# Mean squares of a fused transformer block: square sums turned by TensorE and added up by VectorE

## Chip, cores, metric

One core of one Trainium2 chip. The metric is the device time of one launch, in microseconds; the median of the runs is compared. PE is TensorE, DVE VectorE, ACT ScalarE, POOL GpSimd.

## The reference

128 sequences of 64 tokens with 256 features pass a conditioned layer norm, attention with 16 heads and a gated feed-forward network. Two of its steps are RMS norms, one ahead of attention and one ahead of the network:

```
xhat = layernorm(x) * w + b + tanh(cond @ lin_w.T + lin_b);  x = xhat * w + b
norm(x, t) = gamma(t) * x * rsqrt(mean(x * x, axis=-1) + 1e-6) + beta(t)
x = x + a_alpha(t) * attention(norm_a(x, t))
x = x + f_alpha(t) * swiglu(norm_f(x, t))
```

## The kernel before

The 8192 tokens are worked on in 32 parts of 256 tokens (four sequences). Features lie on the partitions (two halves of 128, `KT`), tokens along the free axis. All engines run one static list of slots `s` from -8 on. A slot does one sequence of attention scores (`s`), the exponentials, the turned probabilities of sequence `s-2`, the product with the values of `s-3`, and one quarter (step `f = s - 12`) of the feed-forward work of a part. Four slots make a group (`grp = s // 4`, `j = s % 4`); each engine goes through the list in order, and semaphores tie them together.

The norms of two parts share the group: part `grp + 2` for attention and part `grp - 2` for the network. Groups -2 to 1 have the first only, groups 2 to 29 both, groups 30 to 33 the second only. Their way:

- j = 0: TensorE turns the input of part `grp + 2` (`turn_x`, L310, four transposes). VectorE makes the residual (L576). ACT squares both parts (L763, L769), POOL adds the two feature halves (L949, L955), so that `square_sum_a` and `square_sum_f` are 128 partitions x 256 tokens.
- j = 1: `mean_squares` (L318, L323): for each block of 128 tokens a product with the square sums as the stationary operand and the column `mean_col` (all 1/256) as the moving one, which leaves the mean of each token on a partition, in columns 0 to 3 of `norm_bank`. VectorE adds epsilon to the 128 x 4 numbers (`mean_squares_out`, L626) and signals `ms_out`; POOL raises them to -1/2 (`inverse_rms`, L942).
- j = 2: `spread_inverses` (L331): one transpose per block of a column broadcast along 128, after which `norm_bank` holds the inverse of each token on all partitions; VectorE multiplies with it (`scale_by_rms`, L629).

`norm_bank` is PSUM bank 1, the bank that `hidden` fills in every slot from 12 on. So TensorE waits in `norm_bank_read` for whoever reads the bank for the norm before `hidden` writes it: at j = 1 for `ms_out`. Large products are done as three fp32r products of high and low halves (`three_pass`, L280 to L282).

In the list of TensorE a slot with j = 1 is: `turn_probs` (L408), `times_values` (L419), `score` (L397), `mean_squares`, 12 products of `queries`, 12 of `gate`, 12 of `hidden`, 12 of `down` (L468, L472 to L474; the first of a part is 512 columns wide, L468, and clears the bank). VectorE has in such a slot: `product_lo` (L666), `find_least` (L584), `mean_squares_out` (L626), `gate_ffn` (L674), `activate` (L652, waits for ACT's tanh, L845), `invert_sums` (L600, L605), `product` (L660), and in every second group statistics (L532, L539 to L549). ACT has `probs_out` (L830), then the exponentials (L822, eight), tanh (L845), `queries_out` (L796) and `product_hi` (L851). POOL has `normalise_probs` (L1002), `inverse_rms` (L942), in every second group `normalise_tokens` (L994), and `add_ffn` (L1011).

Of the kernel before, what the change touches and what calls it, by code (L numbers as in the profile page):

```python
# [28 lines left out]
ALU = mybir.AluOpType  # L29
ACT = mybir.ActivationFunctionType  # L30
F32 = mybir.dt.float32
F32R = mybir.dt.float32r
AX_X = mybir.AxisListType.X

P = 128
BATCH, SEQ, D = 128, 64, 256
# [11 lines left out]
NC = 4  # L48
VW = 2 * DH
SCALE = (HEADS / D) ** 0.5  # L50
LN_EPS, RMS_EPS = 1e-5, 1e-6

SHIFT, A_GAMMA, A_BETA, A_ALPHA, F_GAMMA, F_BETA, F_ALPHA = range(7)
# [14 lines left out]
def conditioned_block(nc, x, cond_t, mod_w, feat_vecs, attn_w, gate_w, hidden_w, out_w, identity, head_mask, out_t):  # L68
    with ExitStack() as ctx:
        def sb(name, shape, dt=F32):  # L70
            return ctx.enter_context(nc.sbuf_tensor(name, shape, dt))

        def sem(name):
            return ctx.enter_context(nc.semaphore(name))
# [4 lines left out]
        turn_bank, norm_bank, work = bank[0], bank[1], bank[7]  # L79
# [5 lines left out]
        vecs = sb("vecs", [P, 4, KT])  # L85
        w_sq = sb("w_sq", [P, KT])
        ident = sb("ident", [P, P])
        mean_col = sb("mean_col", [P, 1])
        minus_half = sb("minus_half", [P, TILES])
        mask = sb("mask", [P, 4])  # L90
        pair = sb("pair", [P, 2])
# [13 lines left out]

        squares_a = sb("squares_a", [P, KT, PART])
        square_sum_a = sb("square_sum_a", [P, PART])
        mean_sq = sb("mean_sq", [P, 4])
        normed_a = sb("normed_a", [P, KT, PART])
        xn_hi = sb("xn_hi", [P, KT, PART], F32R)  # L110
# [9 lines left out]
        probsT = [sb(f"probsT{i}", [P, NC * P]) for i in range(2)]  # L120
# [4 lines left out]
        squares_f = sb("squares_f", [P, KT, PART])  # L125
        square_sum_f = sb("square_sum_f", [P, PART])
# [24 lines left out]
        stats_made, merged, var_made, rstd_made = sem("stats_made"), sem("merged"), sem("var_made"), sem("rstd_made")  # L151
        x_normed, x_turned, res_made = sem("x_normed"), sem("x_turned"), sem("res_made")
        squared_a, sq_sum_a, squared_f, sq_sum_f = sem("squared_a"), sem("sq_sum_a"), sem("squared_f"), sem("sq_sum_f")
        ms_mm, ms_out, inv_made, inv_spread = sem("ms_mm"), sem("ms_out"), sem("inv_made"), sem("inv_spread")
        gamma_a, scaled_a, xn_a = sem("gamma_a"), sem("scaled_a"), sem("xn_a")
        hi_a, lo_a = sem("hi_a"), sem("lo_a")
        k_mm, k_out, q_mm, q_out, v_mm, v_out = (sem("k_mm"), sem("k_out"), sem("q_mm"), sem("q_out"),
# [15 lines left out]
        def is_part(m):  # L173
            return 0 <= m < NPART

        def is_seq(g):
            return 0 <= g < BATCH
# [7 lines left out]
        def is_group(grp):  # L185
            return is_part(grp + 2) or is_part(grp - 2)

        def norm_step(s):
            return 3 if s == -2 else 2 if s == -1 else s % PSEQ
# [16 lines left out]
        def res_part(m):  # L206
            return x_res[:, m // 2 % RES, :, m % 2 * PART:(m % 2 + 1) * PART]
# [70 lines left out]
        def _(pe):  # L278
# [12 lines left out]
            def norm_bank_read(j, grp):  # L291
                if j == 0 and is_part(grp + 2):
                    pe.wait_ge(res_made, 2 * (grp + 2) + 2)
                if j == 1 and is_group(grp):
                    pe.wait_ge(ms_out, grp + 3)
                if j == 2 and is_part(grp + 2):
                    pe.wait_ge(scaled_a, grp + 3)
                if j == 2 and is_part(grp - 2):
                    pe.wait_ge(scaled_f, grp - 1)

            def norm_bank_free(s):
                norm_bank_read(norm_step(s - 1), (s - 1) // PSEQ)
                if s - FFN_AT >= 1:
                    pe.wait_ge(prod_made, min(s - FFN_AT, FFN_STEPS))
# [6 lines left out]
                                          xin[m // 2 % 2][:, m % 2 * 2 + i, kt * P:(kt + 1) * P], ident[:])  # L311
                mm.then_inc(x_turned, 1)

            def mean_squares(grp):
                if is_part(grp + 2):
                    pe.wait_ge(sq_sum_a, grp + 3)
                    for i in range(2):
                        mm = pe.matmul(norm_bank[:, i:i + 1], square_sum_a[:, i * P:(i + 1) * P], mean_col[:],  # L318
                                       start=True, stop=True)
                if is_part(grp - 2):  # L320
                    pe.wait_ge(sq_sum_f, grp - 1)
                    for i in range(2):
                        mm = pe.matmul(norm_bank[:, 2 + i:3 + i], square_sum_f[:, i * P:(i + 1) * P], mean_col[:],  # L323
                                       start=True, stop=True)
                mm.then_inc(ms_mm, 1)

            def spread_inverses(grp):
# [28 lines left out]
            def queries(m):  # L356
                if m >= 1:
                    pe.wait_ge(k_out, m + 1)
                project(WQ, m).then_inc(q_mm, 1)
# [22 lines left out]
            def score_banks_free(s):  # L382
                if is_seq(s - 1):
                    pe.wait_ge(scores_read, s)
                if s % PSEQ == 3 and is_part(s // PSEQ - 1):
                    pe.wait_ge(att_lo_made, s // PSEQ)
# [14 lines left out]
            def turn_probs(g):  # L401
                pe.wait_ge(probs_made, g + 1)
                if g >= 1:
                    pe.wait_ge(probsT_out, g)
                if g + 2 - FFN_AT >= 1:
                    pe.wait_ge(act_made, g + 2 - FFN_AT)
                for r in range(4):
                    mm = pe.transpose(turn_bank[:, r * P:(r + 1) * P], probs[g % 2][:, r * P:(r + 1) * P], ident[:])  # L408
                mm.then_inc(probs_turned, 1)
# [72 lines left out]
            for s in range(FIRST_SLOT, LAST_SLOT):  # L482
                grp, j, f = s // PSEQ, s % PSEQ, s - FFN_AT
                if is_seq(s - 2):
                    turn_probs(s - 2)
                score_banks_free(s)
                if is_seq(s - 3):
                    times_values(s - 3)
                if is_seq(s):
                    score(s)  # L490
                norm_bank_free(s)
                if j == 0 and is_part(grp + 2):
                    turn_x(grp + 2)
                if norm_step(s) == 1 and is_group(grp) and s >= 0:
                    mean_squares(grp)
                if norm_step(s) == 2 and is_group(grp) and s >= -4:
                    spread_inverses(grp)
                if s == FIRST_SLOT + 1:
                    mean_squares(grp)
                if s == FIRST_SLOT + 2:  # L500
                    spread_inverses(grp)
                if s == FIRST_SLOT + 1:
                    pe.wait_ge(rest_loaded, 16)
                    modulation(A_BETA, 2)
                if s == FIRST_SLOT + 2:
                    modulation(F_GAMMA, 3)
                if s == 0:
                    values(0)
                if j == 0 and is_part(grp + 1):
                    keys(grp + 1)  # L510
                if j == 1 and is_part(grp + 1):
                    queries(grp + 1)
                if s == FIRST_SLOT + 5:
                    mean_squares(grp)
                if j == 2 and 1 <= grp + 1 < NPART:
                    values(grp + 1)
                if j == 3 and is_part(grp - 1):
                    attention_out(grp - 1)
                if is_step(f):
                    gate(f)  # L520
                    hidden(f)
                if is_step(f - 1):
                    down(f - 1)

        @block.vector
        def _(dve):
# [94 lines left out]
            def mean_squares_out(grp):  # L621
                dve.wait_ge(ms_mm, grp + 3)
                if grp >= -1:
                    dve.wait_ge(inv_spread, grp + 2)
                cols = norm_cols(grp, 1)
                dve.tensor_scalar(mean_sq[:, cols], norm_bank[:, cols], RMS_EPS, None, ALU.add).then_inc(ms_out, 1)  # L626

            def scale_by_rms(normed, first):
                return dve.tensor_tensor(normed[:], normed[:],  # L629
# [76 lines left out]
            for s in range(FIRST_SLOT, LAST_SLOT):  # L706
                grp, j, f = s // PSEQ, s % PSEQ, s - FFN_AT
# [50 lines left out]
        def _(act):  # L758
            def square_a(m):
                act.wait_ge(res_made, 2 * m + 2)  # L760
                if m >= 1:
                    act.wait_ge(sq_sum_a, m)
                act.activation(squares_a[:], res_part(m), ACT.Square).then_inc(squared_a, 1)  # L763

            def square_f(m):
                act.wait_ge(resid_made, m + 1)
                if m >= 1:
                    act.wait_ge(sq_sum_f, m)
                act.activation(squares_f[:], res_part(m), ACT.Square).then_inc(squared_f, 1)  # L769

            def split_hi_a(m):
                act.wait_ge(xn_a, m + 1)
# [19 lines left out]
            def queries_out(m):  # L792
                act.wait_ge(q_mm, m + 1)
                if m >= 2:
                    act.wait_ge(scored, PSEQ * (m - 1))
                act.activation(q_heads[:, m % 2].rearrange("p k s t -> p (k s t)"), proj_bank(WQ, m), ACT.Copy, scale=-SCALE  # L796
                               ).then_inc(q_out, 1)
# [69 lines left out]
                    act.activation(split_cols(w_hi, w), raw_weight(w), ACT.Copy).then_inc(w_hi_made, 1)  # L867

            act.wait_ge(consts_set, 1)
            act.activation(probsT[0][:, 0:1], mean_col[:], ACT.Tanh)  # L870
            act.wait_ge(loaded, 16 * 3)
            act.wait_ge(mod_mm, 1)
            for kt in range(KT):
# [7 lines left out]
            for s in range(FIRST_SLOT, LAST_SLOT):  # L881
                grp, j, f = s // PSEQ, s % PSEQ, s - FFN_AT
# [45 lines left out]
        def _(pool):  # L928
# [81 lines left out]
                pool.wait_ge(gated_f_made, m + 1)  # L1010
                pool.tensor_tensor(res_part(m), res_part(m), gated_f, ALU.add).then_inc(y_made, 1)  # L1011

            pool.memset(mean_col[:], 1.0 / D)
            pool.memset(minus_half[:], -0.5).then_inc(consts_set, 1)
            pool.memset(v_diag[:], 0.0).then_inc(v_cleared, 1)
            pool.wait_ge(consts_set, 1)
# [1 line left out]
            for s in range(FIRST_SLOT, LAST_SLOT):  # L1018
                grp, j, f = s // PSEQ, s % PSEQ, s - FFN_AT
# [72 lines left out]
```

## Time and profile before

| | |
|---|---|
| runs | 1029.57 us median of 3 (1027.64 to 1029.68) |
| profiled execution | 1028.54 us, span 1026.7 us, mean granted clock 0.985 |
| busy | PE 986.7 us (96%), DVE 668.0 (65%), ACT 624.8 (61%), POOL 565.1 (55%) |

Times are microseconds from the start of the span. The busy time of PE includes the pipelines' depth, so the start of the next instruction is what tells the cost of one. Rows are quoted as the profile and the trace give them.

### The profile page before, as it was taken

How to read it: one execution, taken by the hardware profiler on the slowest of the kernel's cores; microseconds unless marked ns; L12 is line 12 of the kernel's file. 1: busy time of each engine (PE TensorE's matmuls, PEld its weight loads, DVE VectorE, ACT ScalarE, POOL GpSimd, SP SyncE). 2: the span in 40 equal slices, each digit the busy share in tenths (PEclk: the TensorE clock that was granted, in tenths of full speed). 3: DMA queues.
4: the chain of work that ended last, by engine and by line, in shares of the span. 5: the costliest groups of instructions: out<-in, count | busy, mean ns of one | idle time of the engine just before them, and what ended most of it. 6: DMA issues, size and time to landing. Idle time of an engine off the chain costs nothing.

```text
span 1026.7 us, 28723 instructions
## 1 busy us (share of the span) xinstructions
PE 986.7 (96%) x11292; PEld 923.9 (90%) x11292; DVE 668.0 (65%) x1311; ACT 624.8 (61%) x1775; POOL 565.1 (55%) x532
## 2 busy tenths in 40 slices
PE   5677999999999999999999999999999999999997
PEld 5566999999999999999999999999999999998897
DVE  5566666666666666666666666666666666666554
ACT  4566565666666666666666666666666666666432
POOL 4476646565474656547465654746565474443320
PEclk9788999999999999999999999999999999999999
DMA  6100001000100100010000001000000000000000
GB/s 206 43 21 22 2 11 33 11 23 12 32 12 11 33 11 23 11 33 12 12 33 12 23 11 34 11 12 33 12 23 12 12 12 12 12 11 13 11 12 21
DMA packets 20917, 23.37 MB, mean 23 GB/s; under 512 B 1200, under 2 KB 20272, under 8 KB 20784
## 3 DMA queue, kind: packets, MB, share of 16 engines
q1 hardware_dynamic: 20784, 21.54, 6.6%
q8 instruction: 91, 1.49, 0.6%
q14 instruction: 42, 0.34, 0.1%
HBM read 13.15 MB, written 8.39 MB: 21 GB/s over the span
## 4 chain that ended last, share of the span: by engine, by line
PE 85%; issue 5%; DVE 4%; ACT 4%; POOL 2%; DMA 0%; POOLq 0%; SPq 0%; ACTq 0%; DVEq 0%
PE psum L280 17%; PE psum L282 16%; PE psum L281 16%; PE psum L474 5%; PE psum L473 5%; PE psum L472 5%; PE psum L408 5%; PE psum L397 4%; PE psum L419 4%; PE psum L331 2%; PE psum L318 2%; ACT probs L822 2%; PE psum L310 1%; PE psum L323 1%; DVE least L584 1%
## 5 line engine op out<-in xcount | busy, mean ns | idle before, releaser
L280 PE MATMUL psum<-xf_hi,ffn_hi 128*128 128x256 f32 x1024 | 288.3, 282 | 2.8 <-DVE normed_f L629 1.6
L281 PE MATMUL psum<-xf_lo,ffn_hi 128*128 128x256 f32 x1024 | 286.4, 280 | 0.0
L282 PE MATMUL psum<-xf_hi,ffn_lo 128*128 128x256 f32 x1024 | 285.5, 279 | 0.0
L822 ACT ACTIVATE probs<-psum,least 128x64 f32<-128x64 f32 x976 | 212.1, 329 | 53.5 <-DVE least L584 30.1
L652 DVE SCALAR_TENSOR_TENSOR late<-tanh,psum 128x512 f32<-128x512 f32 x128 | 88.0, 688 | 223.7 <-ACT tanh L845 223.7
L1002 POOL TENSOR_TENSOR probs<-probs,inv_sum 128x512 f32<-128x512 f32 x128 | 139.5, 1090 | 108.3 <-DVE inv_sum L605 107.9
L280 PEld LDWEIGHTS psum<-xf_hi,ffn_hi 128*128 128x128 f32 x1024 | 192.8, 188 | 3.7 <-issue 3.7
L851 ACT ACTIVATE prod_hi<-late 128x512 fp32r<-128x512 f32 x128 | 80.7, 631 | 187.9 <-DVE late L660 185.7
L281 PEld LDWEIGHTS psum<-xf_lo,ffn_hi 128*128 128x128 f32 x1024 | 193.1, 189 | 0.0
L282 PEld LDWEIGHTS psum<-xf_hi,ffn_lo 128*128 128x128 f32 x1024 | 192.7, 188 | 0.0
L474 PE MATMUL psum<-prod_hi,ffn_lo 128*128 128x256 f32 x512 | 143.2, 280 | 0.0
L473 PE MATMUL psum<-prod_lo,ffn_hi 128*128 128x256 f32 x512 | 143.0, 279 | 0.0
L472 PE MATMUL psum<-prod_hi,ffn_hi 128*128 128x256 f32 x480 | 134.2, 280 | 0.9 <-DVE prod_lo L666 0.9
L666 DVE TENSOR_TENSOR prod_lo<-late,prod_hi 128x512 fp32r<-128x512 f32 x128 | 88.6, 692 | 69.1 <-ACT prod_hi L851 68.8
L845 ACT ACTIVATE tanh<-psum 128x512 f32<-128x512 f32 x128 | 81.1, 633 | 44.1 <-PE psum L282 44.1
L988 POOL TENSOR_TENSOR normed_f<-normed_f,mod 128x512 f32<-128x512 f32 x32 | 33.4, 1043 | 118.4 <-DVE normed_f L629 118.4
L474 PEld LDWEIGHTS psum<-prod_hi,ffn_lo 128*128 128x128 f32 x512 | 96.2, 188 | 1.5
L473 PEld LDWEIGHTS psum<-prod_lo,ffn_hi 128*128 128x128 f32 x512 | 96.2, 188 | 0.0
L600 DVE TENSOR_REDUCE row_sum<-probs 128x8 f32<-128x512 f32 x128 | 86.9, 679 | 13.9 <-ACT probs L822 8.3
L472 PEld LDWEIGHTS psum<-prod_hi,ffn_hi 128*128 128x128 f32 x480 | 90.2, 188 | 1.1 <-issue 1.1
L584 DVE TENSOR_REDUCE least<-psum 128x8 f32<-128x512 f32 x128 | 87.7, 685 | 2.9 <-PE psum L397 0.9
L660 DVE TENSOR_TENSOR late<-psum,late 128x512 f32<-128x512 f32 x128 | 87.2, 681 | 2.3 <-PE psum L282 1.1
(102 smaller groups left out, 2246.8 us busy)
## 6 DMA issues: line engine op xcount, KB each, us to landing
out_t_dram<-x_res SPq DMA_DIRECT2D x32, 256.0 KB, 2.1
xin<-x_dram SPq DMA_DIRECT2D x15, 512.0 KB, 3.8
w_raw<-attn_w_dram SPq DMA_DIRECT2D x1, 1024.0 KB, 7.1
x_res<-gate_w_dram SPq DMA_DIRECT2D x1, 1024.0 KB, 9.9
late<-hidden_w_dram SPq DMA_DIRECT2D x1, 1024.0 KB, 11.9
x_res<-out_w_dram SPq DMA_DIRECT2D x1, 1024.0 KB, 5.5
xin<-x_dram SPq DMA_DIRECT2D x2, 256.0 KB, 3.0
k_heads<-mod_w_dram SPq DMA_DIRECT2D x1, 320.0 KB, 5.0
```

Source lines behind the costliest of these rows:

```text
L280: pe.matmul(out, stat_hi, mov_hi, start=first, stop=False)
L281: pe.matmul(out, stat_hi, mov_lo, start=False, stop=False)
L282: return pe.matmul(out, stat_lo, mov_hi, start=False, stop=last)
L472: pe.matmul(out, ffn_hi[:, 2, cols], hi, start=False, stop=False)
L473: pe.matmul(out, ffn_hi[:, 2, cols], prod_lo[f % 2][:, tok], start=False, stop=False)
L474: mm = pe.matmul(out, ffn_lo[:, 2, cols], hi, start=False, stop=q == 3 and mt == KT - 1 and u == 1)
L584: dve.tensor_reduce(least[g % 2][:].rearrange("p (r a) -> p r a", r=4), scores, AX_X, ALU.min).then_inc(least_made, 1)
L652: dve.scalar_tensor_tensor(out=act_gate, in0=tanh[:], scalar=1.0, in1=gate_bank, op0=ALU.add, op1=ALU.mult).then_inc(act_made, 1)
L660: dve.tensor_tensor(prod, hidden_bank, act_gate, ALU.mult).then_inc(prod_made, 1)
L666: dve.tensor_tensor(prod_lo[f % 2][:], prod, prod_hi[f % 2][:, 0:BLK].bitcast(F32), ALU.subtract).then_inc(prod_lo_made, 1)
L822: op = act.activation(probs[g % 2][:, h * SEQ:(h + 1) * SEQ], scores[:, h // 2, h % 2], ACT.Exp, bias=least[g % 2][:, h:h + 1], scale=-1.0)
L1002: pool.tensor_tensor(by_head, by_head, inv_sum[g % 2][:].unsqueeze(2).broadcast_to([P, 8, SEQ]), ALU.mult).then_inc(probs_made, 1)
```

## The change

The column product goes. `turn_squares` transposes each block of 128 tokens of the square sums into a quarter of `norm_bank`; VectorE adds up the 128 columns of each block in one `tensor_reduce` into a new small tile `square_mean`, signals the new semaphore `ms_read` (for which TensorE now waits before it writes the bank), waits for it itself, and adds epsilon from `square_mean` to `mean_sq`. The factor 1/256 moves into ACT's squaring as `scale=ROOT_D`, with D ** -0.5 = 1/16 ahead of the square. `mean_col` is replaced by a two-column tile `warm` for the table-loading tanh.

```
-                    pe.wait_ge(ms_out, grp + 3)
+                    pe.wait_ge(ms_read, grp + 3)
...
-            def mean_squares(grp):
+            def turn_squares(grp):
                 if is_part(grp + 2):
                     pe.wait_ge(sq_sum_a, grp + 3)
                     for i in range(2):
-                        mm = pe.matmul(norm_bank[:, i:i + 1], square_sum_a[:, i * P:(i + 1) * P], mean_col[:],
-                                       start=True, stop=True)
+                        mm = pe.transpose(norm_bank[:, i * P:(i + 1) * P], square_sum_a[:, i * P:(i + 1) * P], ident[:])
                 if is_part(grp - 2):
                     pe.wait_ge(sq_sum_f, grp - 1)
                     for i in range(2):
-                        mm = pe.matmul(norm_bank[:, 2 + i:3 + i], square_sum_f[:, i * P:(i + 1) * P], mean_col[:],
-                                       start=True, stop=True)
+                        mm = pe.transpose(norm_bank[:, (2 + i) * P:(3 + i) * P], square_sum_f[:, i * P:(i + 1) * P], ident[:])
                 mm.then_inc(ms_mm, 1)
...
-                dve.tensor_scalar(mean_sq[:, cols], norm_bank[:, cols], RMS_EPS, None, ALU.add).then_inc(ms_out, 1)
+                dve.tensor_reduce(square_mean[:, cols], norm_bank.rearrange("p (n c) -> p n c", c=P)[:, cols], AX_X, ALU.add
+                                  ).then_inc(ms_read, 1)
+                dve.wait_ge(ms_read, grp + 3)
+                dve.tensor_scalar(mean_sq[:, cols], square_mean[:, cols], RMS_EPS, None, ALU.add).then_inc(ms_out, 1)
...
-                act.activation(squares_a[:], res_part(m), ACT.Square).then_inc(squared_a, 1)
+                act.activation(squares_a[:], res_part(m), ACT.Square, scale=ROOT_D).then_inc(squared_a, 1)
...
-                act.activation(squares_f[:], res_part(m), ACT.Square).then_inc(squared_f, 1)
+                act.activation(squares_f[:], res_part(m), ACT.Square, scale=ROOT_D).then_inc(squared_f, 1)
...
-            act.activation(probsT[0][:, 0:1], mean_col[:], ACT.Tanh)
+            act.activation(warm[:, 1:2], warm[:, 0:1], ACT.Tanh)
...
-            pool.memset(mean_col[:], 1.0 / D)
+            pool.memset(warm[:], 1.0 / D)
```

## Rows read from the trace of the kernel before

**Rows 1.** The windows view, by stretch: busy us (instructions) of each engine, granted clock, DMA share, GB/s.

```profile
core 0: us, PE busy (x) PEld busy (x) DVE busy (x) ACT busy (x) POOL busy (x), PEclk, DMA share, GB/s
40.00:102.00 62.00, 45.85 (x567) 38.95 (x566) 42.06 (x87) 39.95 (x112) 38.62 (x38) 0.84 0.06 18
110.00:920.00 810.00, 810.00 (x9510) 762.16 (x9509) 541.26 (x1052) 519.99 (x1512) 473.52 (x439) 1.00 0.06 18
920.00:962.00 42.00, 40.13 (x484) 37.03 (x483) 26.65 (x48) 24.39 (x75) 15.13 (x15) 1.00 0.03 8
```

**Rows 2.** The page's chain that ended last, by engine.

```profile
PE 85%; issue 5%; DVE 4%; ACT 4%; POOL 2%; DMA 0%; POOLq 0%; SPq 0%; ACTq 0%; DVEq 0%
```

**Rows 3.** The chain in order of time, 500 to 540: start, us, what.

```profile
516.29 0.44 PE psum L408 x4
...
523.18 0.12 PE psum L473
...
523.77 0.44 PE psum L408 x4
...
530.33 0.23 PE psum L468
...
531.86 0.44 PE psum L408 x4
...
539.25 0.44 PE psum L408 x4
```

**Rows 4.** The timeline of PE, slot with j = 1: start, us, instruction.

```profile
524.90 0.61 PE L318 MATMUL psum<-mean_col,square_sum_a 128*128 128x1 f32 x4
525.37 0.58 PE L323 MATMUL psum<-mean_col,square_sum_f 128*128 128x1 f32 x4
525.82 0.36 PE L280 MATMUL psum<-xn_hi,w_hi 128*128 128x256 f32 x1
```

**Rows 5.** The timeline of PE, slot with j = 0.

```profile
517.42 0.66 PE L310 MATMUL psum<-ident,xin 128*128 128x128 f32 x4
517.83 0.37 PE L280 MATMUL psum<-xn_hi,w_hi 128*128 128x256 f32 x1
```

**Rows 6.** The timeline of PE, 523 to 527.5: transposes of the probabilities.

```profile
523.61 0.60 PE L408 MATMUL psum<-ident,probs 128*128 128x128 f32 x4
524.14 0.43 PE L419 MATMUL psum<-probsT,v_diag 128*32 128x64 f32 x16
```

**Rows 7.** The timeline of DVE, slot with j = 1; in brackets the idle time before.

```profile
525.85 0.68 DVE L584 TENSOR_REDUCE least<-psum 128x8 f32<-128x512 f32 x1
526.45 0.15 DVE L626 TENSOR_SCALAR mean_sq<-psum 128x4 f32<-128x4 f32 x1
526.52 0.86 DVE L674 SCALAR_TENSOR_TENSOR late<-psum,vecs,mod 128x256 f32<-128x256 f32 x2
529.59 0.69 DVE L652 SCALAR_TENSOR_TENSOR late<-tanh,psum 128x512 f32<-128x512 f32 x1 [2.21 <-ACT tanh L845]
530.19 0.68 DVE L600 TENSOR_REDUCE row_sum<-probs 128x8 f32<-128x512 f32 x1
530.91 0.20 DVE L605 RECIPROCAL inv_sum<-row_sum 128x8 f32<-128x8 f32 x1
```

**Rows 8.** The timeline of ACT, the same slot.

```profile
528.96 0.60 ACT L845 ACTIVATE tanh<-psum 128x512 f32<-128x512 f32 x1 [0.65 <-PE psum L282]
```

**Rows 9.** Waits of ACT, 110 to 890: total us, times, longest.

```profile
ACT tanh L845 <- PE psum L282: 23.3, 26, 1.1
```

**Rows 10.** The timeline of POOL, the same slot and the next.

```profile
525.36 1.47 POOL L1002 TENSOR_TENSOR probs<-probs,inv_sum 128x512 f32<-128x512 f32 x1
526.79 1.02 POOL L942 TENSOR_TENSOR mean_sq<-mean_sq,minus_half 128x4 f32<-128x4 f32 x1
...
531.19 1.04 POOL L1002 TENSOR_TENSOR probs<-probs,inv_sum 128x512 f32<-128x512 f32 x1 [0.89 <-DVE inv_sum L605]
```

**Rows 11.** A line of DVE: duration in ns, least, median, greatest.

```profile
L541 DVE TENSOR_TENSOR merge<-stats x17: 148/153/1016, 6.2 to 816.6; 128x4 f32<-128x4 f32 x15, 128x2 f32<-128x2 f32 x2
```

**Rows 12.** The timeline of PE: starts of the slots 13 and 14.

```profile
102.36 0.63 PE L408 MATMUL psum<-ident,probs 128*128 128x128 f32 x4 [1.77 <-DVE late L652]
...
111.98 0.60 PE L408 MATMUL psum<-ident,probs 128*128 128x128 f32 x4
```

**Rows 13.** The chain in order of time, both ends of the launch.

```profile
79.62 0.58 PE psum L318 x4
80.20 0.45 PE psum L323 x4
...
968.57 0.54 PE psum L323 x4
...
988.89 0.34 PE psum L323 x4
```

**Rows 14.** Who waited for L626, over the whole launch: us, times.

```profile
  PEld psum L331: 1.7, 1
```

More of the change, by code:

```diff
@@ L50 @@
 SCALE = (HEADS / D) ** 0.5
+ROOT_D = D ** -0.5
 LN_EPS, RMS_EPS = 1e-5, 1e-6
@@ L87, in conditioned_block @@
         ident = sb("ident", [P, P])
-        mean_col = sb("mean_col", [P, 1])
+        warm = sb("warm", [P, 2])
         minus_half = sb("minus_half", [P, TILES])
@@ L107, in conditioned_block @@
         square_sum_a = sb("square_sum_a", [P, PART])
+        square_mean = sb("square_mean", [P, 4])
         mean_sq = sb("mean_sq", [P, 4])
@@ L153, in conditioned_block @@
         squared_a, sq_sum_a, squared_f, sq_sum_f = sem("squared_a"), sem("sq_sum_a"), sem("squared_f"), sem("sq_sum_f")
-        ms_mm, ms_out, inv_made, inv_spread = sem("ms_mm"), sem("ms_out"), sem("inv_made"), sem("inv_spread")
+        ms_mm, ms_read, ms_out = sem("ms_mm"), sem("ms_read"), sem("ms_out")
+        inv_made, inv_spread = sem("inv_made"), sem("inv_spread")
         gamma_a, scaled_a, xn_a = sem("gamma_a"), sem("scaled_a"), sem("xn_a")
@@ L494, in _ @@
                 if norm_step(s) == 1 and is_group(grp) and s >= 0:
-                    mean_squares(grp)
+                    turn_squares(grp)
                 if norm_step(s) == 2 and is_group(grp) and s >= -4:
@@ L498, in _ @@
                 if s == FIRST_SLOT + 1:
-                    mean_squares(grp)
+                    turn_squares(grp)
                 if s == FIRST_SLOT + 2:
@@ L513, in _ @@
                 if s == FIRST_SLOT + 5:
-                    mean_squares(grp)
+                    turn_squares(grp)
                 if j == 2 and 1 <= grp + 1 < NPART:
```

## The prediction

> **What bounds the kernel now.** I read the windows view first, cut by stretches. From 110 to 920 us TensorE is busy 810.00 of 810.00 us at the full clock, while VectorE is busy 541, ScalarE 520 and GpSimd 474 us [rows 1]. Before 102 us (slots without the feed-forward network) it is busy 46 of 62 us, and from 920 to 962 us 40 of 42; there other engines decide. The chain that ended last lies 85% on TensorE [rows 2]. So in four fifths of the launch a microsecond taken from TensorE's list is a microsecond of the launch, as long as no other cycle is close behind, and work added to VectorE costs nothing where it sits in an idle stretch. Those two conditions are the whole prediction.
>
> The chain in order of time then gives the slots, counted from one L408 to the next [rows 3]: 7.48 us for j = 0, 8.09 us for j = 1 and 7.39 us for j = 2. Each holds 48 large products. The first and the last have four transposes beside them (the input, the inverses) where j = 1 has the square products; j = 1 also has one 512-wide product (L468, 0.23 us where the others take 0.12). A group of four slots lasts 29.97 us throughout this stretch.
>
 The replacement does not exist in this place, but its form does: four fp32 transposes, each one record, of blocks of 128 x 128 in SBUF with the same identity. In the slot before, in the same place behind the scores, they cost 517.83 - 517.42 = 0.41 us [rows 5]. The difference is 0.51 us per group with both parts. The slots check it from outside: against j = 0 it is 8.09 - 7.48 - 0.11 (L468) = 0.50 us. Bounds: the dearest transposes, at the head of a slot, take 524.14 - 523.61 = 0.53 us for four [rows 6], which leaves a gain of 0.39; against the slot j = 2 it would be 8.09 - 7.39 - 0.11 = 0.59 [rows 3]. I take 0.51, as the nearest row has the same place, type, size and source.
>
> **What it adds to VectorE.** Before, one operation on four columns, 0.15 us long, with the next one starting 0.07 us after it. After, a `tensor_reduce` of 128 x 512 from PSUM: L584 has this form, 0.68 us, next start after 0.60 [rows 7]. Then VectorE waits for its own result; L600 and L605 are this pair, 0.72 us from start to start. Then the addition again, 0.07 to its successor. Added: 0.72 us per group with both parts, half the columns and some 0.45 us with one. Cover: in j = 1 VectorE does `gate_ffn` (to 527.38) and then idles 2.21 us until tanh is done [rows 7]. TensorE reaches the end of `gate` 0.51 us earlier, so the idle time shrinks to 2.21 - 0.51 - 0.72 = 0.98 us: still covered. Without the cover, the 0.72 us would be on the cycle priced under the rivals.
>
> Who else waits for that point? `hidden` on TensorE needs the bank read (`ms_read`). The reduce ends at 526.45 + 0.68 = 527.13, and `hidden` starts 24 products of 0.12 us after `mean_squares`, at about 528.7, or 528.2 after the change: 1.1 us to spare. The waiting signal also comes from the reduce, not from the addition behind it. `gate_ffn` frees the bank of `down`; it ends at 528.1 in place of 527.4, and L468 is due at 530.33 less 0.51. GpSimd's `inverse_rms` starts some 0.5 us later than at 526.79, since `normalise_probs` ahead of it ends at 526.83 [rows 10]; behind it wait `add_ffn` and the next `normalise_probs`, which has 0.89 us of idle time ahead of it, and whose result TensorE needs a slot later. `spread_inverses` needs the inverses at 533, five microseconds on. ScalarE's squares get a scale factor, and the memset and the warming tanh a changed tile: nothing, same instruction, same size; tanh has a scale factor and takes 0.60 us for 128 x 512 [rows 8].
>
> **Ends of the launch.** Both-part groups 3 to 29, that is 27, have their j = 1 slot between 102 and 920 us: 27 x 0.51 = 13.8 us. Group 2's products are on the chain [rows 13]; another 0.5. Groups 30, 32 and 33 turn one part, on the chain, 0.25 each: 0.75. Group 31 lies in the stretch after 920 us that VectorE and ScalarE bound: nothing. Groups -2 to 1: TensorE gains some tenths, the reduce of 256 columns gives them back; only once does the way VectorE, GpSimd, TensorE show as a wait (1.7 us at L331) [rows 14]. I take 0, with 0.8 us either way. Sum: 15.1 us.
>
> **Two rules against the trace.** The granted clock is 1.00, the level of 2.4 GHz, all through the 810 us, and every slot of it holds at least four transposes, every second one eight [rows 1, 3, 5, 6]. The Trainium skill, in "TensorE: Matmul & The Clock Gate", Part 4 (PE-mode transpose), says that transposes don't count as activity for the clock as matmuls do, which speaks against turning products into transposes; by it TensorE might fall to its lower level in j = 1. The trace doesn't bear it out for this mix, and only the exchange in j = 1 is new; it is rival C.
>
> A VectorE operation of four columns took up to 1.016 us where its median is 0.153 [rows 11], so small operations between SBUF tiles are at times held up. The Trainium skill, in "SBUF — State Buffer", section "Who interferes with whom", says that such an operation can be locked out by GpSimd for a whole instruction, while a `tensor_reduce` can't. The old addition read PSUM, the new one reads SBUF: that is the new exposure, 0.86 us at most by the row. In the steady groups GpSimd's next instruction waits for this very addition, so it should not be met there.
>
> **The rivals.** A, the other cycle takes over. VectorE and ScalarE run one of their own through tanh, gelu, sums, product, its halves, least, exponentials and again tanh. In the group at 524 us it waits for TensorE 0.65 us ahead of tanh [rows 8]; over 26 groups these waits sum to 23.3 us, 0.90 each, the longest 1.1 [rows 9], so groups with statistics have 0.65 and the others about 1.15. The cycle alone needs 29.97 - 0.65 = 29.32 us in the former; TensorE will need 29.46. It holds, by 0.14 us. If the new VectorE work lies on this cycle after all (say `find_least` came behind it), the groups with statistics gain nothing (0.65 - 0.72) and the others 0.43: 13 x 0.43 less 13 x 0.07 is 4.7 us, plus 1.2 at the ends, some 1023. Against it: exponentials wait for `find_least`, which is ahead of the reduce.
>
> B, slower: the VectorE work outlasts its cover. Of the 2.21 us of idle time 0.65 are the cycle's own wait for TensorE, so 1.56 us of added work are free even for the cycle; with 0.90 us of waiting in the mean, the group grows beyond 29.97 us from 1.56 + 0.90 = 2.46 us on, and that is where this rival decides. The addition held up by 0.86 makes 1.58 us, which still fits. A reduce that takes three times 0.68 us, because it reads a bank while TensorE writes others, makes 0.72 + 1.36 + 0.86 = 2.94 us: 0.48 too much, 27 times, 13 us, about 1042. L584 reads PSUM beside a writing TensorE and takes 0.68, which speaks against it.
>
> C, slower: the clock falls in j = 1. A slot with the clock low for part of it is slot 13, from 102.36 to 111.98, 9.62 us [rows 12] against 8.09: 1.53 us. Once a group that is 27 x 1.53 = 41 us less 15, about 1055.
>
> D, nothing changes: the transposes cost what the products did (0.92 us for four). No row is near it; 1029.
>
> **Chances.** The forecast 0.84, A 0.06, B 0.03, C 0.03, D 0.04. The profiled execution took 1028.54 us, 1.8 us beyond its span; less 15.1 it is 1013.4. The median of the runs is 1029.57, 1.0 above it, which gives 1014.5; I say 1014.0. Low end: 27 x 0.59 + 1.25 + 0.8 = 18.0 us from 1028.54, 1010.5. High end: 27 x 0.39 + 0.9 - 0.8 = 10.6 us from 1029.57, 1019.0. The cases beyond hold less than 2 in 10, so the range is 1010.5 to 1019. No change that can be told means within 0.2%, 2 us. Faster: forecast and A, 0.90; same: D, 0.04; slower: B and C, 0.06.
>
> **What would show it.** Right: L318 and L323 as two records each, so 64 fewer on either line, with 0.4 us from the first to the following L280; a slot j = 1 of 7.6 us and a group of 29.46; a reduce of 0.68 us and the addition 0.72 behind it; ahead of tanh a wait of 0.15 us in groups with statistics and 0.6 in the others; TensorE busy all the time from 110 us on. Wrong: no wait ahead of tanh and an idle TensorE at L408 or at `hidden` (A, B); a granted clock under 1.00 between 110 and 900 us (C); L310-like starts that are 0.9 us apart (D).

## The result and the profile after

The changed kernel takes 1015.74 us in the median of four runs (1012.19 to 1016.51), the kernel before 1028.93 us in those runs. The ratio is 0.9871, with a 95% interval from 0.9853 to 0.9890: 13.2 us faster. One execution of e1 below, of ten, ran at a mean granted clock of 0.558 and took 1557.73 us; it is in no comparison. The prediction was 1014.0 us, in a range from 1010.5 to 1019.0, with a chance of 0.90 for faster; the sum behind it was 15.1 us.

The windows view of the changed kernel, two stretches, with the columns of [rows 1]:

```profile
102.00:110.00 8.00, 8.00 (x94) 7.52 (x93) 5.58 (x11) 4.48 (x13) 4.16 (x4) 1.00 0.01 3
110.00:900.00 790.00, 790.00 (x9308) 742.59 (x9307) 553.76 (x1068) 517.46 (x1504) 471.43 (x436) 1.00 0.06 18
```

TensorE is still busy all the time, at the same full clock, and VectorE has got busier: 554 us in 790, where it had 541 in 810 [rows 1].

The timeline of PE in the changed kernel, a slot with j = 1, to be read beside [rows 4]:

```profile
484.76 0.44 PE L321 MATMUL psum<-ident,square_sum_a 128*128 128x128 f32 x2
485.03 0.38 PE L325 MATMUL psum<-ident,square_sum_f 128*128 128x128 f32 x2
485.17 0.37 PE L283 MATMUL psum<-xn_hi,w_hi 128*128 128x256 f32 x1
```

From the first transpose to the next product it is 485.17 - 484.76 = 0.41 us, where the square products took 0.92: the 0.51 us of the prediction, to the hundredth. (The lines of `three_pass` are now L283 to L285, the turned probabilities L409.)

The timeline of DVE in a group with statistics, beside [rows 7], then the line of ACT that belongs to it, beside [rows 8], and that of a group without statistics:

```profile
515.18 0.68 DVE L585 TENSOR_REDUCE least<-psum 128x8 f32<-128x512 f32 x1
515.78 0.68 DVE L627 TENSOR_REDUCE square_mean<-psum 128x4 f32<-128x512 f32 x1
516.50 0.17 DVE L630 TENSOR_SCALAR mean_sq<-square_mean 128x4 f32<-128x4 f32 x1
516.58 0.88 DVE L678 SCALAR_TENSOR_TENSOR late<-psum,vecs,mod 128x256 f32<-128x256 f32 x2
518.47 0.69 DVE L656 SCALAR_TENSOR_TENSOR late<-tanh,psum 128x512 f32<-128x512 f32 x1 [1.01 <-ACT tanh L849]
```

```profile
488.29 0.60 ACT L849 ACTIVATE tanh<-psum 128x512 f32<-128x512 f32 x1 [0.62 <-PE psum L285]
...
517.84 0.60 ACT L849 ACTIVATE tanh<-psum 128x512 f32<-128x512 f32 x1 [0.18 <-PE psum L285]
```

The reduce takes 0.68 us, the addition starts 0.72 behind its start, and `gate_ffn` 0.08 later. VectorE still idles 1.01 us before the gelu operation (2.21 before, 0.98 predicted), and the cycle of VectorE and ScalarE still waits 0.18 us for TensorE ahead of tanh in this kind of group and 0.62 in the other (predicted 0.15 and 0.6). The work added to VectorE is hidden whole, with little to spare.

The chain in order of time of the changed kernel, the starts of five slots, beside [rows 3]; the slot from 483.62 is j = 1:

```profile
483.62 0.44 PE psum L409 x4
...
491.20 0.44 PE psum L409 x4
...
498.65 0.43 PE psum L409 x4
...
505.72 0.44 PE psum L409 x4
...
513.17 0.44 PE psum L409 x4
```

Slot j = 1 has 7.58 us (8.09 before), j = 2 7.45, j = 3 7.07, j = 0 7.45, the group 29.55. One more row of before is wanted here, from the same view: with 516.29 of [rows 3] it gives its slot j = 3.

```profile
509.28 0.44 PE psum L408 x4
```

So before, j = 2 and j = 3 took 7.39 and 7.01 us. **Each got 0.05 to 0.06 us longer in the changed kernel**, though nothing in TensorE's list for them is changed and it waits for nobody; j = 0 lost 0.03. From the start of slot 14 to that of slot 118 are 26 groups. They take 779.40 us before and 768.20 after, 29.98 and 29.55 each: of the 0.51 us only 0.43 arrive. That is what the experiments had to explain.

The span of the profiled execution went from 1026.7 to 1010.4 us, 16.3 us, which is more than the medians say. The 26 groups are 11.2 of it, and behind them both executions need 135.3 us. The other 5.0 us lie ahead: slot 13 took 7.6 us in place of 9.62 [rows 12], and it began at 99.3 in place of 102.4. The changed kernel had the full clock there (1.00 from 102 to 110 us, above); the windows view of before, the same stretch, has a mean of 0.79, with the clock at its lower level for part of it:

```profile
102.00:110.00 8.00, 7.64 (x77) 7.24 (x78) 3.07 (x8) 4.26 (x14) 6.01 (x6) 0.79 0.02 3
```

Slot 13 goes by this clock in all profiles but those with added reduces. At a mean of 1.00 in the slot it took 7.6 us with the cheap squares (the changed kernel, e7) and 8.1 to 8.2 with the column products (e1b, p3); at 0.81 or 0.82 it took 9.0 to 9.6 (e2, p1, e3, before), at 0.69 it took 11.1 (p2). So some 1.5 of its 2.0 us are the clock of that one execution and 0.5 the change. It was the shortest of the four runs; the other three took 1015.03 to 1016.51. The start differs by some microseconds between executions, and the medians are the better guide.

### The profile page after: what moved, and what is told of

It is laid out like the page before. It is cut to its first block, busy times and chain, and to the rows that moved or that the text cites. A ratio compares the mean times of both kernels' runs of the same rounds, so it can differ in the third digit from the quotient of the medians.

```text
span 1010.4 us, 28503 instructions
## 1 busy us (share of the span) xinstructions
PE 964.5 (95%) x11164; PEld 900.0 (89%) x11164; DVE 691.4 (68%) x1347; ACT 625.8 (62%) x1775; POOL 565.9 (56%) x532
## 4 chain that ended last, share of the span: by engine, by line
PE 86%; DVE 5%; issue 4%; ACT 3%; POOL 1%; DMA 0%; POOLq 0%; SPq 0%; ACTq 0%; DVEq 0%
PE psum L283 17%; PE psum L285 16%; PE psum L284 16%; PE psum L475 6%; PE psum L474 6%; PE psum L473 5%; PE psum L409 5%; PE psum L398 4%; PE psum L420 4%; PE psum L332 2%; PE psum L313 2%; ACT probs L826 2%; PE psum L321 1%; DVE least L585 1%; PE psum L469 1%
## 5 line engine op out<-in xcount | busy, mean ns | idle before, releaser
L283 PE MATMUL psum<-xf_hi,ffn_hi 128*128 128x256 f32 x1024 | 287.5, 281 | 4.2 <-DVE normed_f L633 1.6
L285 PE MATMUL psum<-xf_hi,ffn_lo 128*128 128x256 f32 x1024 | 285.9, 279 | 0.0
L283 PEld LDWEIGHTS psum<-xf_hi,ffn_hi 128*128 128x128 f32 x1024 | 192.2, 188 | 5.7 <-issue 4.4
L285 PEld LDWEIGHTS psum<-xf_hi,ffn_lo 128*128 128x128 f32 x1024 | 192.4, 188 | 0.0
L1006 POOL TENSOR_TENSOR probs<-probs,inv_sum 128x512 f32<-128x512 f32 x128 | 139.7, 1091 | 76.7 <-DVE inv_sum L606 76.2
```

Of the source, the lines that this page charges most:

```text
L283: pe.matmul(out, stat_hi, mov_hi, start=first, stop=False)
L285: return pe.matmul(out, stat_lo, mov_hi, start=False, stop=last)
L1006: pool.tensor_tensor(by_head, by_head, inv_sum[g % 2][:].unsqueeze(2).broadcast_to([P, 8, SEQ]), ALU.mult).then_inc(probs_made, 1)
```

## Experiments

Group lengths below are read from the starts of the slots in each kernel's own profile, in the steady stretch. First, each half of the change alone.

**e1: the reduce alone.** The products with the column stay.

```
+                dve.tensor_reduce(square_mean[:, cols], norm_bank.rearrange("p (n c) -> p n c", c=P)[:, cols], AX_X, ALU.add
+                                  ).then_inc(ms_read, 1)
+                dve.wait_ge(ms_read, grp + 3)
                 dve.tensor_scalar(mean_sq[:, cols], norm_bank[:, cols], RMS_EPS, None, ALU.add).then_inc(ms_out, 1)
```

> The kernel before (products with the column kept) with VectorE's new work added: the reduce over norm_bank into square_mean, the wait for it, then the old addition. The sums that the reduce makes are not used. Theory (VectorE's 0.72 us lie in its idle time): a group stays 29.97 us, ratio 1.000 within 0.002. Rival 1 (the new work is on the cycle of VectorE and ScalarE): groups of 30.04 and more, with no wait left ahead of tanh. Rival 2 (the reduce slows TensorE's products beside it, which would explain why the changed kernel's slots j = 2 and j = 3 are 0.05 us longer each than before): slots of 7.45 and 7.06 where before has 7.39 and 7.01, a group of 30.06.

The ratio was 1.0038 (1.0021 to 1.0055), nine executions of 1029.47 to 1032.81 us: 4 us slower, outside what I expected. The profile of the same kernel is e1b.

> The same kernel as e1_reduce_only once more, for a profile at full clock. e1 measured 1.0038 of before. Theory (VectorE's new work is hidden, and what e1 lost is the pace of TensorE's products): slots of 7.45 to 7.46 and 7.06 for j = 2 and 3 as in the changed kernel, j = 0 and j = 1 as before, a group of 30.06, TensorE without a wait from 110 us on, and a wait ahead of tanh that is still 0.5 us or more. Rival (hidden only in part): TensorE idle at L408 or at hidden in some slots.

The chain in order of time of e1b, starts of slots; the slot from 493.37 is j = 1:

```profile
485.91 0.44 PE psum L410 x4
...
493.37 0.44 PE psum L410 x4
...
501.45 0.44 PE psum L410 x4
...
508.90 0.44 PE psum L410 x4
...
515.97 0.44 PE psum L410 x4
```

The slots take 7.46, 8.08, 7.45 and 7.07 us, the group 30.05, as the theory had it. TensorE has no wait from 110 us on, and the waits ahead of tanh sum to 23.9 us over 26 groups, against 23.3 before [rows 9]. VectorE's work is hidden, and yet j = 2 and j = 3 have got their 0.05 to 0.06 us. This execution took 1029.55 us, beside 1029.86 of before: a single pair of executions doesn't resolve 2 us.

**e2: the transposes alone.** VectorE reads one column of each turned block, so the sum is left out. TensorE waits for `ms_out` again, as before.

```
-                dve.tensor_reduce(square_mean[:, cols], norm_bank.rearrange("p (n c) -> p n c", c=P)[:, cols], AX_X, ALU.add
-                                  ).then_inc(ms_read, 1)
-                dve.wait_ge(ms_read, grp + 3)
-                dve.tensor_scalar(mean_sq[:, cols], square_mean[:, cols], RMS_EPS, None, ALU.add).then_inc(ms_out, 1)
+                dve.tensor_scalar(mean_sq[:, cols], norm_bank.rearrange("p (n c) -> p n c", c=P)[:, cols, 0], RMS_EPS, None,
+                                  ALU.add).then_inc(ms_out, 1)
```

> The changed kernel without the reduce: the square sums are turned, but VectorE adds epsilon to one column of each turned block, so the sum over features is left out. Theory (all of the gain is TensorE's 0.92 less 0.41 us): slot j = 1 of 7.58 us, a group of 29.46 to 29.55, the same time as the changed kernel within 0.2%. If the reduce is what lengthens the slots j = 2 and 3, they are 7.39 and 7.01 and the group is 29.46, some 2.5 us faster than the changed kernel; if it is anything else, 7.45 and 7.06 and 29.55. Rival (the reduce costs time on the way to tanh): 5 us or more faster than the changed kernel.

Ratio 0.9857 (0.9827 to 0.9887), median 1012.71 us. The slots are 7.58, 7.45, 7.06 and 7.46, the group 29.55. Taking the reduce away does not bring back the 0.08 us. So the lost pace appears with either half of the change, and neither half is needed for it. All of the gain is TensorE's.

**e3: the transposes doubled.**

```
                     for i in range(2):
-                        mm = pe.transpose(norm_bank[:, i * P:(i + 1) * P], square_sum_a[:, i * P:(i + 1) * P], ident[:])
+                        for _ in range(2):
+                            mm = pe.transpose(norm_bank[:, i * P:(i + 1) * P], square_sum_a[:, i * P:(i + 1) * P], ident[:])
...
```

> The changed kernel with each transpose of the square sums issued twice into the same place. Theory (TensorE's list sets the group, and a transpose costs about 0.11 us there): slot j = 1 of 7.58 + 4 x 0.11 = 8.02 us, a group of 29.99, time near 1027 to 1028. Rival (transposes overlap with the products behind them and cost less): under 7.8 us for the slot. Rival (the cycle of VectorE and ScalarE already sets the group): the group stays 29.55.

The chain of e3, one slot with j = 1:

```profile
492.90 0.44 PE psum L411 x4
...
500.91 0.44 PE psum L411 x4
```

8.01 us, 0.43 more for four more transposes (0.11 each), a group of 29.97, 1027.77 us. The price lies in full on the path that sets the end, and at 110 to 900 us the clock stays at its upper level with eight transposes beside the four of the probabilities in one slot.

**e7: column products of one pass.**

```
-        square_sum_a = sb("square_sum_a", [P, PART])
+        square_sum_a = sb("square_sum_a", [P, PART], F32R)
...
+        mean_col_r = sb("mean_col_r", [P, 2], F32R)
...
-                        mm = pe.matmul(norm_bank[:, i:i + 1], square_sum_a[:, i * P:(i + 1) * P], mean_col[:],
+                        mm = pe.matmul(norm_bank[:, 2 * i:2 * i + 2], square_sum_a[:, i * P:(i + 1) * P], mean_col_r[:],
```

> The kernel before with the square sums and the column rounded to fp32r (two equal columns in place of one): four products of one pass each, no reduce. It loses bits of the sums. Theory (what the column products cost is their number of passes and weight loads, eight of 0.115 us): slot j = 1 of 7.6 us, within 0.05 of the changed kernel, group 29.46 to 29.55. Rival (transposes are cheap for another reason, and a product costs more whatever its pass): slot of 7.8 or more.

The timeline of PE in e7:

```profile
487.30 0.38 PE L320 MATMUL psum<-mean_col_r,square_sum_a 128*128 128x2 f32 x2
487.55 0.36 PE L325 MATMUL psum<-mean_col_r,square_sum_f 128*128 128x2 f32 x2
487.77 0.36 PE L282 MATMUL psum<-xn_hi,w_hi 128*128 128x256 f32 x1
```

0.47 us for four products with four weight loads, where eight took 0.92. Slot j = 1 has 7.61 to 7.66 us, the group 29.53, the time 1014.24 us. So what the old products cost was their number of passes. A transpose (0.41 for four) is no cheaper kind of product beyond 0.015 us apiece; it does a full-precision block in one instruction. The slots j = 2, 3 and 0 of e7 are 7.39, 7.01, 7.48 in one group and 7.41, 7.06, 7.44 in the next.

**e4, e4b and e5: how much cover VectorE has.** The first two repeat the reduce; e4b has `range(4)`. In e5 the two operations are ahead of `find_least`.

```
+                for n in range(2):
+                    dve.tensor_reduce(square_spare[:, n, cols], norm_bank.rearrange("p (n c) -> p n c", c=P)[:, cols], AX_X,
+                                      ALU.add)
```

> The changed kernel with the reduce done three times (two of them into a spare tile), 1.2 us more of VectorE work per group. Theory (VectorE idles 1.45 us ahead of the gelu operation in groups without statistics and about 1.0 with them, and the cycle has 0.15 us more to give): the groups with statistics exceed their cover by some 0.1 us, which the buffers between the engines even out; group 29.55 to 29.62, time within 2 us of the changed kernel. Rival (VectorE work counts in full): 27 x 1.2 = 32 us slower.

> The changed kernel with the reduce done five times, 2.4 us more per group, 3.12 in all beyond before. The prediction put the point from which a group exceeds 29.97 us at 2.46 us. Theory: 29.97 + 3.12 - 2.46 = 30.6 us per group, time about 1045, slower than before, with TensorE waiting at hidden (for ms_read) or at L409, and no wait left ahead of tanh. Rival (more slack than I count): under 1030.

```
+                if j == 1 and is_group(grp):
+                    mean_squares_out(grp)
                 if is_seq(s):
                     find_least(s)
                     if wide(s):
                         centre(s)
                 if j == 0 and is_part(grp + 2):
                     make_residual(grp + 2)
-                if j == 1 and is_group(grp):
-                    mean_squares_out(grp)
```

> The changed kernel with the reduce and the addition ahead of find_least in VectorE's list. Nothing is added; the 0.72 us and a short wait for the turned squares now lie ahead of the exponentials, on the cycle of VectorE and ScalarE. Theory (rival A's price): groups with statistics 30.0 to 30.2 us, the others 29.55 to 29.7, time 1021 to 1025. Rival (the cycle is slacker than I count): same as the changed kernel.

e4 took 1033.66 us, 16 us more than the theory allows, with groups of 30.05 in the mean. A good part of that is in slots that have no added work and in which TensorE waits for nobody: 7.52, 7.15 and 7.51 us for j = 2, 3 and 0, together 0.22 above the changed kernel. In 11 of the 26 groups j = 2 takes 7.84, and there TensorE is held at `hidden` (its first product comes 0.35 us behind the one before it, where 0.12 is usual), since VectorE's `scale_by_rms` reads the bank late. The theory of the cover failed for the sum, and the pace of the products was again in it, stronger.

e4b took 1059.56 us, its group 30.88. Here the waits view shows TensorE waiting itself, at `hidden`, for the reduce:

```profile
PE psum L284 <- DVE square_mean L631: 25.7, 26, 1.6
```

That a group grows beyond 29.97 us came out, but the 2.46 us are not the limit that it met. They come from the idle time ahead of tanh. The nearer limit is the bank: by the prediction's own figures the reduce may end 1.1 us later before `hidden` needs the bank, so the cover is 0.72 + 1.1 = 1.82 us, and e4b's 3.12 are 1.3 above it. In the timeline the first product of `hidden` comes 1.06 us behind the one before it in groups without statistics, 1.44 in the others. Of the 15 us by which the time is off, 0.28 x 26 = 7.3 lie in the groups, the rest ahead of slot 14 and behind slot 118.

In e5, the timeline of DVE, a group with statistics:

```profile
521.05 0.68 DVE L627 TENSOR_REDUCE square_mean<-psum 128x4 f32<-128x512 f32 x1
521.76 0.29 DVE L630 TENSOR_SCALAR mean_sq<-square_mean 128x4 f32<-128x4 f32 x1
521.97 0.68 DVE L585 TENSOR_REDUCE least<-psum 128x8 f32<-128x512 f32 x1
```

`find_least` starts 0.92 us later than it could, on the cycle through exponentials and tanh, and the waits view has no wait ahead of tanh any more. The groups change between 29.4 and 30.0, the mean is 29.69, the time 1019.72 us: 4 us lost by the place of two operations in a list. TensorE pays at `hidden` in slots with j = 2, whose first product comes up to 0.5 us behind the one before it. Rival A's mechanism is real, at about half of the price that I gave it (1023).

**p1 to p4: the place of the tiles.** The kernels that lost pace have one thing in common: a new small tile, `square_mean`, in the middle of the list of allocations. If each tile is placed behind the last and takes up a multiple of 32 bytes, everything behind it lies 32 bytes further on in each partition in the changed kernel, in e1, e2, e3 and e5, 32 + 32 = 64 bytes in e4 and 32 + 64 = 96 in e4b; e7 has a shift by 32 further up the list, which takes the weights along. `warm` takes the 32 bytes that `mean_col` had. The step of 32 is a reading of mine; p2 (32 bytes declared, the slots of e1b with its 16) and p3 (64 declared, the slots of e4) agree with it. p1 moves that one line, and changes no instruction:

```
-        square_mean = sb("square_mean", [P, 4])
         mean_sq = sb("mean_sq", [P, 4])
...
         prod_lo = [sb(f"prod_lo{i}", [P, BLK], F32R) for i in range(2)]
+        square_mean = sb("square_mean", [P, 4])
```

> The changed kernel with the small tile square_mean allocated behind all others, so that every tile after it lies where it lay before the change (in the changed kernel they lie 32 bytes further on). No instruction changes. The lost 0.09 us per group were there with the reduce alone and with the transposes alone, and both of those kernels have the new tile. Theory (the place of the operands sets the pace of TensorE's products): slots j = 2 and 3 of 7.39 and 7.01 again, j = 1 of 7.58, a group of 29.46, which is 27 x 0.09 = 2.4 us faster than the changed kernel, ratio to before 0.984 to 0.986. Rival (the pace comes from when the other engines work): 7.45 and 7.06 as in the changed kernel, ratio 0.987.

The chain in order of time of p1; the slot from 485.93 is j = 1:

```profile
485.93 0.44 PE psum L409 x4
...
493.50 0.44 PE psum L409 x4
...
500.92 0.44 PE psum L409 x4
...
507.93 0.44 PE psum L409 x4
...
515.41 0.44 PE psum L409 x4
```

7.57, 7.42, 7.01 and 7.48 us, a group of 29.48: the 7.01 of before is back, and half of what j = 2 had lost (7.39 to 7.45). Median 1013.13 us, ratio 0.985 (0.983 to 0.987). That is 0.2% better than the changed kernel's ratio, with intervals that overlap; the slots of the profile are what tells them apart.

p2 and p3 are the kernel before with a tile that nobody uses:

```
+        spare = sb("spare", [P, 8])
         mean_sq = sb("mean_sq", [P, 4])
```

> The kernel before with one unused tile of 32 bytes ahead of mean_sq, nothing else: all tiles behind it lie where the changed kernel has them. Theory (place): 7.45, 7.06, a group of 30.05 to 30.06, 2.4 us slower than before, ratio 1.002 to 1.004, as e1 with the reduce. Rival (what e1 lost came from the reduce): 29.97 and ratio 1.000.

Ratio 1.0026 (1.0013 to 1.0038), slots of 7.45, 7.06, 7.46 and 8.08, a group of 30.05: the same slots as e1b, without its reduce. 32 unused bytes cost 2.7 us (1.3 to 3.9 by the interval), of which the groups are 26 x 0.08 = 2.0; e1's 1.0038 needs no other cause, as the two intervals overlap.

> The kernel before with an unused tile of 64 bytes at that place, which is where the tiles lie in e4 (reduce three times). Theory (place): slots of about 7.52, 7.15 and 7.51 for j = 2, 3, 0 as in e4, j = 1 of 8.15, a group of 30.3, about 9 us slower than before, with no VectorE work added. Rival (e4 was slow through its reduces): 29.97.

The chain in order of time of p3 (`[P, 16]` in place of `[P, 8]`); the slot from 497.45 is j = 1:

```profile
482.79 0.44 PE psum L409 x4
...
489.94 0.44 PE psum L409 x4
...
497.45 0.44 PE psum L409 x4
...
505.61 0.44 PE psum L409 x4
...
513.13 0.44 PE psum L409 x4
```

7.15, 7.51, 8.16 and 7.52 us, a group of 30.35, 1038.92 us, with TensorE busy for 810.00 of 810 us. These are e4's slots without any of its work: 64 unused bytes make the kernel some 11 us slower (one execution; the groups alone give 26 x 0.37 = 9.6).

> e4 (reduce three times) with its small tiles allocated last, so the other tiles lie as before the change. Theory (place explains most of e4's 18 us, VectorE's 1.2 us little): a group of 29.46 to 29.65, time 1014 to 1019. Rival (the reduces cost): above 1028.

1019.82 us in place of e4's 1033.66. Groups without statistics have 29.48 us, nothing lost to 1.2 us of added reduces; those with statistics mostly 29.75, with one of 30.15 and one of 30.78, as `hidden` starts some 0.2 us late. The timeline of p4, the reduce on DVE and the first product of `hidden` (522.98) on PE, due 0.12 behind the last of `gate`:

```profile
522.15 0.68 DVE L631 TENSOR_REDUCE square_mean<-psum 128x4 f32<-128x512 f32 x1
...
522.67 0.28 PE L286 MATMUL psum<-xf_hi,ffn_lo 128*128 128x256 f32 x1
522.98 0.36 PE L284 MATMUL psum<-xf_hi,ffn_hi 128*128 128x256 f32 x1
```

The time is 0.8 us above the theory's range. So in the groups with statistics VectorE's cover ends a little under the 1.92 us that p4 adds, and what ends it is the bank that `hidden` needs, at the 1.82 us of above, not the idle time ahead of tanh (0.72 + 0.98 = 1.70 by the prediction). The two limits lie too close to be told apart by the size of the loss; the late start at `hidden` is what shows which one TensorE met.

## Why the prediction was right, and where its sum was off

**What bounds the kernel: right.** e3 adds 0.43 us to TensorE's list and the group grows by 0.43; e1b adds 0.72 us to VectorE's and TensorE still waits for nobody, ScalarE ahead of tanh as long as before. **TensorE, 0.92 - 0.41 = 0.51 us: right**, in slot j = 1 (8.09 to 7.58) and from first transpose to next product; L321 and L325 have 64 records each where L318 and L323 had 128, as foretold. The nearest row, the transposes of the input in the same place, was the right one to price it by. **VectorE, 0.72 us under a cover of 2.21: right**, down to the idle time that was left (0.98 predicted, 1.01 measured).

**The step that was mis-sized is "27 x 0.51 = 13.8 us".** It took the other three slots of a group as untouched. They cost 0.08 us a group more, some 2 us in all, because the change also declared a tile: 27 x 0.43 = 11.6 us, and with 13.2 us measured some 1.6 are left for the ends, where I had 1.25. The ends can't be split further, since launches differ there by more than that: the slot j = 1 of group 30 got 0.28 us shorter (0.25 predicted), but the whole stretch behind slot 118 took 135.3 us before and after. Nothing in the range from 1010.5 to 1019.0 was meant for such a loss; that it fitted in is luck. p1 has no such shift and its group gains 0.49 us. The interval of its ratio stands for 13.4 to 17.5 us (its median is 14.4 below that of before), and the sum of 15.1 lies in it. I had looked at what the diff does to the lists of the engines, and had called its tiles free.

**Rival A** (the cycle takes over) did not come: its waits for TensorE ahead of tanh are still there, in the waits view of the changed kernel from 110 to 870 us:

```profile
ACT tanh L849 <- PE psum L285: 10.2, 25, 0.6
```

0.41 us in the mean of 25 groups, where before had 0.90 [rows 9]. e5 shows what it would have cost. **Rival B** (VectorE outlasts its cover) did not come, with 0.72 us of added work; e4b went there and was slower than before. But its threshold, 2.46 us, left out a limit that the prediction had itself worked out, the 1.1 us to spare at `hidden`: TensorE is held from about 1.8 us on (p4, e4b). The new addition was held up at least once: at 79.5 us it took 0.832 us (median 0.169) and ended 0.02 us behind GpSimd's L1006, which had begun ahead of it. In the steady groups no GpSimd instruction ran beside it, since GpSimd had finished and waited for it. The timeline of POOL beside [rows 10]:

```profile
514.69 1.48 POOL L1006 TENSOR_TENSOR probs<-probs,inv_sum 128x512 f32<-128x512 f32 x1
516.75 1.03 POOL L946 TENSOR_TENSOR mean_sq<-mean_sq,minus_half 128x4 f32<-128x4 f32 x1 [0.58 <-DVE mean_sq L630]
```

**Rival C** (the clock falls) did not come: 1.00 from 110 to 900 us, with eight transposes now in three slots of four. The Trainium skill's rule in "TensorE: Matmul & The Clock Gate", Part 4, is not borne out by this list, in which four to twelve transposes stand beside 48 products in a slot (e3 has the twelve) and the granted clock is 1.00; no run here has a stretch of transposes alone. **Rival D**: the transposes cost 0.41 us, not 0.92.

Not settled: which tile's place counts, and what in the chip minds it. Shown is that the place does it: p1, p2 and p3 move tiles and nothing else. Known are four places of the tiles from `mean_sq` on: as before, 32 and 64 bytes further, with 29.98, 30.05 and 30.35 us per group, and 96 in e4b, whose slots j = 3 and j = 0, with no wait in them, are 7.10 and 7.44 us. So more bytes don't always mean slower. The 36 feed-forward products of a slot j = 3 take 4.21, 4.24 and 4.32 us, 0.117, 0.118 and 0.120 each. Three further observations narrow it down.

- In p3 the starts of these products repeat with a period of six, 0.117, 0.125, 0.116, 0.123, 0.118 and 0.121 us apart, from end to end of the slot, while the instructions of the other engines come and go; that speaks against their accesses as the cause.
- e7 has the large tiles as far on as the changed kernel, and the weights too, so that their distance is that of before; it never shows the changed kernel's 7.45, 7.06 and 7.45, and in 13 of 26 groups those of before to 0.01 us. That speaks for distances between tiles and against the moving tile's own place, but e7 has other instructions too, and no run moves the weights alone.
- One placement can have several paces. Before has 7.06 in place of 7.01 for j = 3 in one group of 26, and e5, placed as the changed kernel, has 6.85 in six, with products 0.113 us apart, each time behind a slot j = 2 that was longer than 7.45 us because TensorE was held at `hidden`. The chain of e5, a slot j = 3 of this kind:

```profile
296.45 0.44 PE psum L409 x4
...
303.30 0.44 PE psum L409 x4
```

## What to carry to other kernels

Where one engine is busy without a gap, count its instructions and price the new ones by the nearest row in the same place. What goes to another engine is free as long as three things hold: the idle time there, less what the gain itself takes from it, covers it; it stands behind the operation on which the next cycle depends; and the bank or buffer that it reads is still free in time for whoever writes it next. Work out each of these limits and take the least. An fp32 product with one column took two passes with two weight loads here (0.92 us for four); a transpose of the same block took one (0.41 for four), and the sum can be had elsewhere. Put a new small tile behind the large ones, or look at the slots that should not have changed: when they did and nobody waits in them, suspect the places of the tiles, and test that with an unused tile.

## What the runs showed of the hardware that was not expected

- TensorE's large products (fp32r, 128 x 128 by 256 columns), back to back and at the upper clock, got slower by 0.3% and 1.2% of a group when their SBUF tiles lay 32 and 64 bytes further on, with the same instructions and no waits (p2, p3 against before). At one placement they can also have more than one pace (0.113 and 0.118 us apart in e5).
- The bank that a reduce reads was the first limit of hidden work on VectorE: at 1.92 us of added work TensorE's next product for that bank started 0.19 us late (p4).
- Slot 13 took 7.6, 9.0 and 11.1 us (the changed kernel, p1, p2) with granted clocks of 1.00, 0.81 and 0.69 in it.
- Four fp32r products of one pass with a two-column moving operand take 0.47 us, four fp32 transposes of 128 columns 0.41 us: the narrow moving operand was no cheaper than the wide one.
